# Conditional attention over 64 tiles on one core: new places for the normalisation of x and the low parts on VectorE, and another order of work at the end

## The reference

```python
h = _layernorm(x)
mod = jax.nn.silu(time) @ mod_w + mod_b
shift, scale, gate = jnp.split(mod, 3, axis=-1)
h = h * (scale + 1.0) + shift
qkv = (h @ w_qkv).reshape(B, T, 3, H, e).transpose(2, 0, 3, 1, 4)
q, k, v = (qkv[0], qkv[1], qkv[2])
q = _apply_rope(_layernorm(q, q_norm_w), position)
k = _apply_rope(_layernorm(k, k_norm_w), position)
scores = jnp.einsum('bhqe,bhke->bhqk', q, k) / jnp.sqrt(jnp.asarray(e, q.dtype))
attn = jax.nn.softmax(scores, axis=-1)
o = jnp.einsum('bhqk,bhke->bhqe', attn, v)
o = o.transpose(0, 2, 1, 3).reshape(B, T, D)
return x + o @ w_out * gate
```

## Time and profile before

| what | value |
| --- | --- |
| median of 3 runs | 1784.97 us (1782.56 to 1785.4) |
| the profiled execution, its own time | 1784.8 us |
| its span, first to last instruction | 1783.0 us |
| PE busy | 1678.6 us (94%) |
| DVE busy | 1274.4 us (71%) |
| ACT busy | 1035.1 us (58%) |
| POOL busy | 635.1 us (36%) |
| mean granted TensorE clock | 0.987 |

### The profile page before, as it was taken

The page is one execution under the profiler, slowest core; times in us unless marked ns, Lnnn a source line. Parts: engine busy times, 40 slices in busy tenths (PEclk is TensorE's granted clock), DMA queues, the critical chain, the costliest instruction groups (busy, mean ns, idle before and its releaser), DMA issues.

```text
span 1783.0 us, 34594 instructions
## 1 busy us (share of the span) xinstructions
PE 1678.6 (94%) x13342; PEld 1010.2 (57%) x13342; DVE 1274.4 (71%) x1667; ACT 1035.1 (58%) x1610; POOL 635.1 (36%) x708
## 2 busy tenths in 40 slices
PE   5978899999999999999999999999999999999987
PEld 3645456555565555655556555565555655555444
DVE  8766677777777777777777777777777777775553
ACT  3445566566556566656655656665665665655552
POOL 0613234334334424433433442442343343243222
PEclk9979999999999999999999999999999999999999
DMA  6034445545455464554645545455554555543554
GB/s 209 25 66 95 101 107 116 128 107 125 113 117 133 101 138 105 119 125 104 139 102 133 117 104 135 106 128 116 119 121 111 124 114 118 123 110 84 124 122 127
DMA packets 55576, 205.53 MB, mean 115 GB/s; under 512 B 6888, under 2 KB 6888, under 8 KB 39160
## 3 DMA queue, kind: packets, MB, share of 16 engines
q0 software_dynamic: 18288, 133.18, 38.4%
q1 hardware_dynamic: 37128, 70.14, 11.7%
HBM read 53.25 MB, written 16.88 MB: 39 GB/s over the span
## 4 chain that ended last, share of the span: by engine, by line
PE 70%; DVE 23%; issue 4%; DMA 1%; POOL 0%; ACT 0%; SPq 0%; DVEq 0%; POOLq 0%; ACTq 0%
PE Y L357 10%; PE O L458 10%; PE SA L439 9%; PE Y L344 8%; DVE xin L1017 7%; DVE cst L1050 7%; PE Y L347 7%; PE Y L351 6%; PE Y L474 6%; PE SM L396 6%; DVE qk_lo L1039 4%; PE SA L443 2%; DVE stats L984 2%; PE SA L334 1%; DVE cst L1058 1%
## 5 line engine op out<-in xcount | busy, mean ns | idle before, releaser
L1050 DVE TENSOR_REDUCE cst<-SM 128x2 fp32r<-128x1024 f32 x236 | 289.3, 1226 | 295.5 <-PE MB L396 295.3
L807 ACT ACTIVATE probs<-SM 128x1024 f32<-128x1024 f32 x256 | 262.4, 1025 | 237.2 <-PE SM L443 230.7
L1298 POOL DMA_DIRECT2D probs<-probs x127 | 111.0, 874 | 690.1 <-ACT probs L809 624.4
L1050 DVE TENSOR_REDUCE cst<-MB 128x2 fp32r<-128x1024 f32 x236 | 287.2, 1217 | 0.0
L458 PE MATMUL O<-probs,vals 128*32 128x512 f32 x2048 | 272.4, 604 | 0.0
L809 ACT ACTIVATE probs<-SA 128x1024 f32<-128x1024 f32 x256 | 262.4, 1025 | 0.0
L1279 POOL TENSOR_TENSOR pair_part<-rows,rope_pair 128x256 f32<-128x256 f32 x128 | 94.5, 739 | 383.9 <-DVE rows L1027 383.0
L344 PE MATMUL Y<-wqkv_hi,hT_hi 128*128 128x512 f32 x716 | 214.9, 422 | 0.0
L347 PE MATMUL Y<-wqkv_hi,hT_lo 128*128 128x512 f32 x716 | 193.8, 392 | 0.4 <-DVE hT_lo L1033 0.4
L351 PE MATMUL Y<-wqkv_lo,hT_hi 128*128 128x512 f32 x716 | 192.2, 390 | 0.0
L703 ACT ACTIVATE rows<-Y 128x512 f32<-128x512 f32 x121 | 72.6, 600 | 205.7 <-PE Y L351 205.7
(11 more groups left out here) (208 smaller groups left out, 3589.9 us busy)
## 6 DMA issues: line engine op xcount, KB each, us to landing
probs<-probs POOLq DMA_DIRECT2D x127, 1024.0 KB, 7.7
xin<-in_x_dram SPq DMA_DIRECT2D x62, 256.0 KB, 7.4
xres<-in_x_dram SPq DMA_DIRECT2D x60, 256.0 KB, 2.6
out_dram<-xres SPq DMA_DIRECT2D x60, 256.0 KB, 5.5
shift_scale<-mod_rows SPq DMA_DIRECT2D x15, 512.0 KB, 3.8
gate<-mod_rows SPq DMA_DIRECT2D x16, 256.0 KB, 5.5
rows<-in_L_cond_mod_w_dram SPq DMA_DIRECT2D x2, 1024.0 KB, 8.9
probs<-in_L_cond_w_qkv_dram SPq DMA_DIRECT2D x2, 1024.0 KB, 13.2
```

The lines of the kernel that those rows point to most:

```text
L807: act.activation(probs[:, a, 2:4, :], SM[:], ACT.Exp).then_inc(s_exp, 1)
L1050: dve.tensor_reduce(heads[:, 2 * half:2 * half + 2, 0], bank[:], AX.X, ALU.max, negate=True).then_inc(max_out, 1)
```

## The change

On VectorE, in every slot: `square_sums(s + 5, 0)` moves from ahead of the two `low_qk(s + 1, ...)` to behind them, and `normalize_x(s + 7)` moves from behind the last maxima of the slot (t = 3) to ahead of them. At the end: the out projection of tile 58 moves from slot 63 to the end of slot 62, and that of tile 59 from behind the loop into slot 63, with ScalarE's `output_high` and GpSimd's `output_low` for them moved ahead too. The accumulating DMA `add_keys(63, 1)` is left out, and the sums of group 63 over its key tile 1 are made by PE, with one more `add_last_sums`. Two thirds of the last projections of tiles 60 and 61 that are possible early (groups 0 and 1) move into slot 63, with tile 61 in bank Y. The four loads of `last_res` are issued ahead of `store(58)`, in slot 63. VectorE's gate of tile 58 and `last_parts` of groups 0 and 1 open slot 63.

```diff
-        last_banks = [MB[:, 1, :], SM[:, 1, :], SA[:, 0, :], SA[:, 1, :]]
+        last_banks = [MB[:, 1, :], Y[:], SM[:, 1, :], SA[:, 0, :]]
...
+                if s == LAST:
+                    sp.wait_ge(qkT_done, 2 * (NS - NG))
+                    for t in range(TT):
+                        sp.dma_start(last_res[t], x_t[NB - 1, t]).then_inc(ld_last[t], 16)
                 if s - 5 >= 0:
                     store(s - 5)
                 if s - 4 >= 0:
                     load_residual(s - 4)
...
+            load_gate(NB - 1)
             store(NT - 5)
-            sp.wait_ge(qkT_done, 2 * NS)
-            for t in range(TT):
-                sp.dma_start(last_res[t], x_t[NB - 1, t]).then_inc(ld_last[t], 16)
-            load_gate(NB - 1)
...
+                    if s == LAST:
+                        pe.wait_ge(y_gated, NT - TT - 1)
                     add_over_keys(s - 1, 0, 1)
                     weigh_values(s - 1, 3)
...
                 weigh_values(s, 0)
+                if s == LAST:
+                    add_last_sums(0)
...
-                n = s - 5
+                n = s - 5 if s < LAST else NT - TT - 1
...
                 weigh_values(s, 1)
+                if s == LAST:
+                    add_last_sums(1)
+                    pe.wait_ge(last_low, 2)
+                    project_last(0, 0, 2)
...
                 weigh_values(s, 2)
+                if s == LAST:
+                    add_last_sums(2)
+                    pe.wait_ge(sum_added, 2 * LAST)
+                    project_last(1, 0, 2)
...
+                if s == LAST - 1:
+
+                    pe.wait_ge(o_low, NT - TT - 1)
+                    pe.wait_ge(first_summed, 2 * s + 1)
+                    project_out(NT - TT - 2, Y[:], 0, 12)
...
-            pe.wait_ge(o_low, NT - 4)
-            pe.wait_ge(y_gated, NT - 5)
-            project_out(NT - 5, Y[:], 0, 12)
-
-            pe.wait_ge(first_added, 16 * NS)
-            for t in (0, 2):
-                add_last_sums(t)
-            pe.wait_ge(last_low, 3)
-            project_last(0, 0, 3)
             weigh_values(LAST, 3)
             add_last_sums(3)
-            for t in range(1, TT):
-                project_last(t, 0, 3)
+            pe.wait_ge(last_low, 3)
+            project_last(0, 2, 3)
+            project_last(1, 2, 3)
+            project_last(2, 0, 3)
+            project_last(3, 0, 3)
             pe.wait_ge(last_low, NG)
...
                 if s > 0:
                     move_o(s - 1)
+                if s == LAST:
+                    output_high(NT - TT - 1)
...
                     inverse_sums(s - 1)
+                if s == LAST - 1:
+                    output_high(s - 4)
...
-                if s - 4 >= 0:
+                if 0 <= s - 4 and s < LAST - 1:
                     output_high(s - 4)
...
             for s in range(LAST + 1):
-                if s > 0 and tile(s + 5):
-                    square_sums(s + 5, 0)
+                if s == LAST:
+                    apply_gate(NT - TT - 2, Y[:], gated[:])
+                    last_parts(0)
+                    last_parts(1)
                 if group(s + 1):
                     low_qk(s + 1, 0)
                     low_qk(s + 1, 1)
+                if s > 0 and tile(s + 5):
+                    square_sums(s + 5, 0)
...
                 if s - 5 >= 0:
-                    apply_gate(s - 5, Y[:], gated[:])
+                    apply_gate(s - 5 if s < LAST else NT - TT - 1, Y[:], gated[:])
...
+                if tile(s + 7):
+                    normalize_x(s + 7)
                 if late(s + 1):
                     late_maxima(s + 1, 3, 0)
                     late_maxima(s + 1, 3, 1)
                 elif group(s + 1):
                     maxima(s + 1, 3)
-                if tile(s + 7):
-                    normalize_x(s + 7)
                 if s == LAST:
-                    last_parts(0)
-                    last_parts(1)
                     last_parts(2)
-                    apply_gate(s - 4, Y[:], gated[:])
...
             for s in range(LAST + 1):
+                if s == LAST:
+                    add_residual(NT - TT - 2)
+                    output_low(NT - TT - 1)
+                    scale_o(s - 1)
+                    add_residual(NT - TT - 1)
+                    break
                 add_keys(s, 1)
...
-                if s < LAST:
-                    add_keys(s, 3)
+                if s == LAST - 1:
+                    output_low(s - 4)
+                add_keys(s, 3)
                 if s - 5 >= 0:
                     add_residual(s - 5)
-                if s - 4 >= 0:
+                if 0 <= s - 4 and s < LAST - 1:
                     output_low(s - 4)
-            add_residual(LAST - 4)
```

## The result

| | before | after |
| --- | --- | --- |
| median | 1785.18 us (4 runs, 1782.56 to 1787.26) | 1738.79 us (4 runs, 1738.36 to 1745.76) |
| profiled execution, span | 1784.8, 1783.0 us | 1738.36, 1736.6 us |
| mean granted clock | 0.987 | 0.988 |

The ratio is 0.975, with an interval of 0.9722 to 0.9778. The change saves 46.4 us, by the medians and by the two spans alike; forecast were 37.3.

A forecast was written before the change was run, and what follows sets the result against it. TensorE, busy 94% of the span, was taken as the bound, waiting for `low_qk` slot after slot. Savings of 34.5 (loop) + 2.8 (end) = 37.3 us from 1784.8 gave 1747.5, as a median 1747.7 us; range 1741 to 1758.

The forecast's parts named there:

- The bound and the two moves: Main loop: TensorE's wait for `low_qk`, 34.5 us in 52 slots, goes entirely once VectorE's `normalize_x` and `square_sums` move.
- The late entry of L1017: Moved `normalize_x`, first half, held through `scale_o` and one rotation step: maxima 0.36 us late, costing 0 to 0.05 us a slot.
- the early entry: Moved `normalize_x` gets in earlier, ahead of or behind `scale_o`: the pair ends at 961.5 to 962.1 and costs nothing.
- The term 32.5 + 2.0 for the loop: TensorE's listed waits for `low_qk`, all saved: 32.5 us in slots 6 to 56, 2.0 us in slot 57.
- The end: Slots 62 and 63: reordered projections bring TensorE's last product 2.8 us earlier, between 1.0 and 5.3.
- T: Start of TensorE's projection in slot 63, put at 1751.2 on the clock of before, between 1748.7 and 1753.0.
- Rivals 1 and 2: VectorE's last maxima late, `transpose_c` waits: 1, half the gain returns, 1766, chance 0.09; 2, slower than before, 1823, chance 0.05.
- Rival 3: Loop: another engine becomes what TensorE waits for, and only the end is gained: 1782, chance 0.04.
- The range: Whole kernel: 1741 to 1758 us, the lower end from savings of 37.2 and 5.3 us, widened for the spread of runs.
- The loop's bound: Upper bound of the loop's saving: 51 slots at 0.69 us, the difference of slots 33 and 5, plus 2.0: 37.2 us.

The follow-up runs named there:

- the kernel with the exchange on GpSimd: Changed kernel with GpSimd's `output_low(59)` put ahead of `add_residual(58)` in slot 63: 1740.01 us, ratio 0.9739; run again, 1740.29 us, ratio 0.9739.
- the second set: Later runs on one chip, in which the changed kernel ran again unaltered: 1745.81 us, ratio 0.9767.
- the four additional instructions: Changed kernel with four extra VectorE statistics instructions, result unused, between `normalize_x` and the last maxima of every slot: 1824.88 us (one run).

## Why the prediction was right and where it was wrong

**The bound and the two moves: right.** The one wait that came back in every slot was the loop's whole loss, and all of it went. `low_qk` found VectorE free, slots have one length, and no wait took its place. Moving `normalize_x` alone would have been enough, which the prediction didn't ask.

**The late entry of L1017: not what happened.** The prediction kept as its bound an L1017 held through `scale_o` and one rotation step, with the pair ending 0.36 us late. In slot 33 L1033 (the former L1017) ran 0.82 us, nearly undisturbed, and it was `scale_o` that lost time; VectorE was idle for 0.96 us between the pair and the last maxima. The Trainium skill ("SBUF — State Buffer", section "Who interferes with whom") gives the shared ports to the one of the two engines that issues first. By that, an L1033 issued at 965.21 runs ahead of a `scale_o` taken up at 965.44, and L1036, taken up at 966.06, waits for it. Here the trace agrees. In the place before, it did not seem to, but the prediction left out a row. When L1017 was taken up, at 964.57, GpSimd was still in the addition ahead of `o_lo`, until 963.56 + 1.58 = 965.14:

```profile
963.56 1.58 POOL L1292 TENSOR_TENSOR xres<-xres,gated 128x512 f32<-128x512 f32 x1
```

So L1017 met two instructions of GpSimd one behind the other, and that row is no clean test of which goes first; why `o_lo` then went ahead of it stays open. For the forecast this means that the early entry, and not the bound, was the right choice; the sum took the cost at 0 by either, so no term of it was off by this.

**What failed.** The forecast of the saving was 9.1 us short (46.4 - 37.3): 4.4 in the loop's term, 4.5 in slots 58 to 61, for which it had no term, and 0.7 in the end's, less 0.5 ahead of slot 6. Two steps failed, then, of about the same size. With the loop at 38.9 alone the forecast would have been 1743.3 us, inside its range; it is with the clock's share that the time fell out of it.

**The term 32.5 + 2.0 for the loop: mis-sized, 38.9 measured.** It took the waits view's total for the time that TensorE loses. The windows above split the gain of slots 6 to 57: idle time fell from 1366.79 - 1332.34 = 34.45 us to 0, which is the 34.5 forecast; but TensorE's *busy* time fell as well, by 1332.34 - 1327.90 = 4.44 us, though it had one product fewer of 10818. The products didn't become faster. While it runs without a break, TensorE starts L397 0.97 us after L459; the record of L459 is 1.04 us long, since ends overlap the next start. Before a wait the overlap of 0.07 us counts as busy time. So a wait listed as 0.63 us holds the next product up by (4.61 - 2.94) - 0.97 = 0.70 us, where 2.94 is 968.02 - 965.08, the start of L458 in slot 33 before; a wait listed as nothing can hold it up by 0.12, as the run with `square_sums` alone showed. The prediction had the difference of slots 33 and 5, 0.69 us, and used it for the bound alone; 51 x 0.70 are 35.7, slot 57 gave 27.64 - 25.54 = 2.1, and the remaining 1.1 us, 0.02 a slot, lie further on in the slots.

**A term put at nothing: 4.5 us in slots 58 to 61.** The prediction has no term for these slots and none for the clock; as work they are indeed untouched. What differed is the granted clock, 0.95 and 1.00 in the two traces. The unaltered kernel had 91.39 us there in another execution, both halves of the change apart had 92.3 to 92.5, and the kernel with the exchange on GpSimd 97.5 and 91.4. So of the 46.4 us some 2 to 4 are the luck of the profiled execution. Since a median of four fell on the same side, it is in the measured median too: in the second set the same kernel's ratio was 0.9767, which against 1784.97 is 1743.4, inside the range.

**The end: right in its mechanism; 3.5 instead of 2.8 us, in part by luck.** T was set by the chain that the prediction named, load, residual, low part. The projection started at 1707.56, which with the 42.9 us that slot 62 starts earlier (1716.49 - 1673.58 = 42.91) is 1750.5 on the clock of before, against 1751.2 forecast; the last product ended at T + 22.9, as forecast. That T came so close is partly luck: the load was issued at 1702.10 + 42.91 = 1745.0, 1.5 us ahead of the forecast's 1746.35 + 0.2, and from there to T it took 5.46 us instead of 4.65. TensorE's wait was 3.1 us where 2 to 3 were named. But the 60.43 us of before hold one spell of the lower clock, and the 56.88 of after none. Against the 58.9 us estimated above for no spell, the new order gave about 2.0 us; the other 1.5 are the clock's. Over all runs the end by itself gave 0.4%, some 7 us, and on top of the two moves nothing that the ratios can tell (0.9765 without it, 0.975 and 0.9767 with it). The five traces with the end of before have one to three spells in slots 62 and 63, the nine with the new end none, but for two with one each. So the new end seems to go with fewer of them; what causes that stays open.

**The rivals.** Rivals 1 and 2 fell: `transpose_c` has no wait for the maxima in slots 6 to 57. Their mechanism is real, as the four additional instructions showed, but the hole had 0.96 us left instead of 0.36 too few. Rival 3 fell too: every slot of the loop lasts 25.53 to 25.54 us.

**The range.** Its lower end put the upper bounds of the loop and the end together, 42.5 us. The loop's bound was 1.7 us too tight, the end stayed within its own, and the clock had no term at all.

## What to carry to other kernels

Where one engine bounds a loop, size a recurring wait by the distance between the starts of the two instructions around it, in a slot with the wait and in one without, and not by the idle time that is listed. Before a difference between two traces is credited to a change, compare the granted clock of the stretch in both. Before an instruction is moved into a hole, find what comes due behind the hole and by how much, since past that point each microsecond costs a whole one in every turn. An instruction that waits for a load should not stand ahead of one on whose result the bounding engine waits: exchanging two lines removed a stall of 3.1 us, and putting `x_low` between two reductions, instead of ahead of or behind both, took 0.75 us off a wait that either other place left at 2.25 to 2.6.

## What the runs showed of the hardware

- TensorE's recorded busy time can hold lost time: 4.44 us of it vanished from slots 6 to 57 with the wait, at the same clock and with one product fewer of 10818. With `square_sums` moved alone, where the hold-up in slot 33 is 0.12 us and 4.78 us are idle in all, it was still there (1332.47 us).
- In slot 33 of after, VectorE's two-input instructions and GpSimd's took turns in whole instructions: 0.82 us for L1033 that got in first, 1.74 for the `scale_o` behind it (1.29 before), 1.66 for L1036 behind that, 1.18 for the rotation step behind L1036. None of these lost more than the length of one instruction of the other engine. In the place before, behind two of GpSimd's, L1017 lost more: it took 2.37 us at the median, where its shortest took 0.74.
- Spells at half the granted clock (0.50, 1.2 GHz) came and went between executions of one program. They lay ahead of the loop, in its first five slots and from slot 57 on, and in none of 14 traces in slots 5 to 56, not even where TensorE waited 1.3 us in each of these. Slot 59 of the kernel after took 22.69 us without one (clock 1.00) and 24.75 with one (0.93); slots 58 to 61, with the same work, took from 89.23 us (1.00) to 97.53 (0.91).
